# A graph network on one core: relational convolutions over (edge tile, block of 128 destinations) pairs, with edge weights found inside the first one

## The reference, cut to what matters

```python
N, E, D, R, L = 6250, 100000, 128, 8, 3          # dst is sorted; src and etype are random
def rgcn_conv(x, src, dst, etype, bases, comp, root, bias):
    weight = einsum('rb,bio->rio', comp, bases)
    h = einsum('ni,rio->nro', x, weight)
    msg = h[src, etype]                           # one row of 128 for each edge
    cnt = segment_sum(ones(E), dst * R + etype, N * R)
    norm = 1.0 / maximum(cnt[dst * R + etype], 1.0)
    return segment_sum(msg * norm[:, None], dst, N) + x @ root + bias
for l in range(L):                                # batch norm and relu between layers
    ...
x = layernorm(x + rgcn)
h = x @ W_in + b_in                               # 64 wide
for _ in range(3):                                # three hops, rows = src, columns = dst
    cur = segment_sum(cur[dst] * edge_weight[:, None], src, N)
x = layernorm(x + (sum of h and the hops) / 4 @ W_out + b_out)
```

## Time and profile before

| | us |
|---|---|
| median of 3 runs (lowest, highest) | 8620.33 (8615.66, 8631.71) |
| the profiled execution | 8602.98 |
| its span, first to last instruction | 8601.2 |
| POOL busy in it | 5966.9 |
| PE busy in it | 6088.5 |
| DVE busy in it | 5032.0 |

### The profile page before, as it was taken

The page is one execution under the profiler, slowest core; times in us unless marked ns, Lnnn a source line. Parts: engine busy times, 40 slices in busy tenths (PEclk is TensorE's granted clock), DMA queues, the critical chain, the costliest instruction groups (busy, mean ns, idle before and its releaser), DMA issues.

```text
span 8601.2 us, 79809 instructions
## 1 busy us (share of the span) xinstructions
PE 6088.5 (71%) x14111; PEld 2066.8 (24%) x14112; DVE 5032.0 (59%) x12874; ACT 793.9 (9%) x2392; POOL 5966.9 (69%) x5856
## 2 busy tenths in 40 slices
PE   7755047777778788777877867777677777677776
PEld 3233012222222222222222221111111111111111
DVE  8977036666646666636666665555555554555556
ACT  5822000000010000020000010000000000000000
POOL 3877776667777667776667647777677777677774
PEclk9955568888888888888888878889889888898998
DMA  5100011111241111241111211111211111211112
GB/s 192 25 4 1 1 26 46 47 46 46 51 130 46 47 46 46 43 141 46 47 46 47 46 32 24 23 23 23 29 23 24 24 23 23 36 23 23 23 24 30
DMA packets 239252, 354.33 MB, mean 41 GB/s; under 512 B 129737, under 2 KB 139802, under 8 KB 238414
## 3 DMA queue, kind: packets, MB, share of 16 engines
q0 software_dynamic: 180352, 239.74, 13.8%
q1 hardware_dynamic: 58396, 109.81, 3.8%
q10 hardware_dynamic: 130, 0.80, 0.0%
HBM read 258.83 MB, written 100.66 MB: 42 GB/s over the span
## 4 chain that ended last, share of the span: by engine, by line
PE 45%; issue 19%; POOL 18%; DVE 8%; another core or an unknown queue 7%; DMA 2%; DVEq 1%; POOLq 0%; ACT 0%; SPq 0%
PE psum L771 43%; POOL placed_src L454 11%; POOL msg L471 7%; DVE sel L1075 2%; DVE agg L1091 2%; DMA msg<-hop_table,stage_idx 2%; PE psum L755 1%; DVEq L1086 1%; DVE bufD L1081 0%; POOL stage_addr L449 0%; DVE bufE L931 0%; DVE node_stats L1152 0%; DVE bufD L1082 0%; DVE cur L1168 0%
## 5 line engine op out<-in xcount | busy, mean ns | idle before, releaser
L771 PE MATMUL psum<-sel,msg 128*128 128x512 f32 (+1 forms) x9672 | 5148.1, 669 | 2117.8 <-issue 1095.7
L1091 DVE TENSOR_TENSOR agg<-agg,psum 128x512 f32 (+1 forms) x2418 | 1642.1, 679 | 3306.5 <-PE psum L771 1607.5
L471 POOL DMA_INDIRECT msg<-hop_table,stage_idx x2418 | 2486.5, 1028 | 1094.6 <-issue 631.5
L471 POOL DMA_INDIRECT msg<-msg_table,stage_idx x2418 | 2414.2, 998 | 1050.3 <-issue 628.1
L771 PEld LDWEIGHTS psum<-sel,msg 128*128 128x128 f32 (+1 forms) x9672 | 1554.0, 177 | 4882.8 <-issue 3752.6
L1075 DVE TENSOR_SCALAR sel<-iota,slots,norm 128x512 f32<-128x512 f32 x2418 | 1304.1, 564 | 12.5 <-ACT agg L576 12.5
L454 POOL DMA_INDIRECT placed_src<-stage_pay,stage_addr x800 | 1022.0, 1278 | 304.9 <-issue 216.2
L1075 DVE TENSOR_SCALAR sel<-iota,slots 128x512 f32<-128x512 f32 x2418 | 1096.5, 492 | 0.1
L505 ACT CAST stage_idx<-slots 128x4 int32<-128x4 f32 x1212 | 232.9, 194 | 6979.9 <-DMA msg<-msg_table,stage_idx 3526.3
L755 PEld LDWEIGHTS psum<-bufD 125*49 125x49 f16 x918 | 95.5, 104 | 842.8 <-issue 683.0
L1122 DVE SCALAR_TENSOR_TENSOR cur<-iota,bufE,psum 128x128 f32<-128x128 f32 x808 | 234.6, 345 | 88.4 <-PE psum L703 56.9
(11 more groups left out here) (176 smaller groups left out, 1613.0 us busy)
## 6 DMA issues: line engine op xcount, KB each, us to landing
msg_table<-sel SPq DMA_DIRECT2D x147, 512.0 KB
msg<-msg_table,stage_idx POOLq DMA_INDIRECT x2418
msg<-hop_table,stage_idx POOLq DMA_INDIRECT x2418
placed_src<-stage_pay,stage_addr POOLq DMA_INDIRECT x800
placed_dst<-edge_rows SPq DMA_DIRECT2D x13, 781.2 KB
hop_table<-sel SPq DMA_DIRECT2D x21, 224.0 KB, 2.8
bufE<-inv_sqrt SPq DMA_DIRECT2D x2, 1568.0 KB, 10.1
out<-cur SPq DMA_DIRECT2D x12, 256.0 KB
```

Source lines behind the costliest of these rows:

```text
L471: g.indirect_dma_start(out=msg[:, b, 0:width], out_offset=None, in_=table, in_offset=bass.IndirectOffsetOnAxis(ap=stage_idx[:, b:b + 1], a ...
L771: t.matmul(psum[0:width, b // 2 % PB, :], msg[:, b, 0:width], sel[:, b % SB, :], start=b % 2 == 0, stop=b % 2 == 1).then_inc(summed, 1)
L1091: v.tensor_tensor(at, at, psum[0:width, q % PB, :], ALU.add).then_inc(added, 1)
```

## The change

The relational convolutions go over visits. The sorted edges stay packed: `NET` = 782 tiles of 128. A visit is a pair of an edge tile and a block of 128 destinations that the tile reaches; a tile that spans a block's end is visited twice, and there are `NV` = 830 visits for any input. `plan_visits` finds each visit's tile and block on DVE and PE; POOL gathers the visits' tiles from `edge_rows` with 7 indirect DMAs. The selection is 128 by 128 (`visit_sel`, 16 buffers), the product 128 columns, four visits to a PSUM bank; each visit is added to `agg` by itself, at a column unpacked from `visit_pack`. The 13 copies by SP are gone, and so is the separate stage of edge weights: in the first convolution DVE makes one-hot rows of the type alone (24 columns), and one instruction (L1182) writes the weighted selection and `norm` together. POOL takes the gather's indices straight from `visit_src`. `CUTS` is now (6, 34, 42, 50): 6 turns, the 7 tile gathers, 28 turns, then 8 and 8 between layers. The histogram of destinations takes 49 steps of DVE in place of 13. The degree steps go with every third visit.

```diff
-CUTS = (38, 44, NSI)
+NET = -(-E // 128)
+NV = NET + NBLK - 1
+MV = 16
+SV = 16
+MAIN = (0, 1, 6)
+CUTS = (6, 34, 42, NSI)
@@ SP
-                for j in range(NB):
-                    sp.dma_start(placed["dst"][bass.ds(to, E), :]...).then_inc(moved, 16)
-                    sp.wait_ge(moved, 16 * (j + 1))
@@ POOL
+            def visit(k):
+                if k == 0:
+                    pool.wait_ge(visits_ready, 1)
+                for v in range(NV):
+                    n = visits(k, v)
+                    if n >= MV:
+                        pool.wait_ge(visit_summed, n - MV + 1)
+                    g.indirect_dma_start(out=msg[:, n % MV, :], out_offset=None, in_=msg_table,
+                                         in_offset=bass.IndirectOffsetOnAxis(ap=visit_src[:, v:v + 1], axis=0)).then_inc(visit_in[n % MV], 16)
...
+            pool.wait_ge(visits_planned, 1)
+            for j in range(VB):
+                g.indirect_dma_start(out=runs[:, j, :, :]..., in_=edge_rows.rearrange("(t e) w -> t (e w)", e=128), ...)
+            place("src", CUTS[0], CUTS[1])
@@ PE
+                for c in range(NQ):
+                    if k == 0:
+                        if c + 2 < NQ:
+                            turn_types(c + 2)
+                        if c + 1 < NQ:
+                            spread_weights(c + 1)
+                    sums(c)
@@ DVE
-            for j in range(NB):
+            for j in range(NBLK):
                 link(v.tensor_scalar(in_bucket, bucket_f, float(j), 0.0, ALU.is_equal, ALU.add, accum_out=hist[:, j:j + 1]))
...
+                def select(c):
+                    if k == 0:
+                        dve.wait_ge(weight_rows, c + 1)
+                    for j, at in enumerate(chunk_of(c)):
+                        if n >= SV:
+                            dve.wait_ge(visit_summed, n - SV + 1)
+                        if k == 0:
+                            v.scalar_tensor_tensor(out=to, in0=iota[:, 0:128], scalar=low, in1=psum[:, 2 + c % 2, j * 128:(j + 1) * 128],
+                                                   op0=ALU.is_equal, op1=ALU.mult, accum_out=norm[:, at:at + 1]).then_inc(visit_ready, 1)
+                        else:
+                            v.tensor_scalar(to, iota[:, 0:128], low, norm[:, at:at + 1], ALU.is_equal, ALU.mult).then_inc(visit_ready, 1)
...
+                def add(c):
+                    columns = block_columns(dve, c)
+                    dve.wait_ge(visit_summed, visits(k, chunk_of(c)[-1]) + 1)
+                    for j, at in enumerate(chunk_of(c)):
+                        if n:
+                            dve.wait_ge(visit_added, n)
+                        to = agg_and[:, bass.ds(columns[j], 128)]
+                        v.tensor_tensor(to, to, psum[:, bank_of(k, c), j * 128:(j + 1) * 128], ALU.add).then_inc(visit_added, 1)
...
-            edge_weights()
```

572 lines of the change are left out of this document (307 added, 265 removed).

## The result

| | kernel before | changed kernel |
|---|---|---|
| median of its runs | 8626.0 us (4 runs) | 8752.7 us (4 runs, 8748.7 to 8763.9) |
| ratio, 95% interval | | 1.0150 (1.0132 to 1.0167) |
| the profiled execution's span | 8601.2 us | 8747.0 us |

The change makes the kernel slower by 1.5%. The prediction was 8465 us, faster, with a range from 8310 to 8730 us: wrong in sign, and the measured time lies outside the range.

What follows compares the result with a forecast made beforehand. POOL was taken as one unbroken chain from 118 us to the third layer's end. Its terms, -103 + 10 - 10 + 102 - 22 - 65 - 67 = -155 us, gave 8448 us profiled, 8465 us as median; range 8310 to 8730 us.

Steps and rivals of the forecast that it cites:

- Placing before the first convolution: Before the first convolution: 64 fewer POOL scatters at 1.60 us each, -103 us.
- disturbance: Before the first convolution: POOL's scatters no longer slowed during the edge-weight stage, -10 us; in each convolution 15 us remain.
- The stage of edge weights is worth nothing: Before the first convolution: removing its 428 us gains nothing by itself, since POOL's scatters run on until 1171 us.
- Boundaries: Between layers: 32 more scatters each time at 1.60 us, hidden by nothing, 51 us twice, +102 us.
- The convolutions: Three layers: 830 gathers at 1.25 us plus disturbance and smaller waits, giving -22, -65 and -67 us.
- DVE's time a visit: In the convolutions: about 1.0 us, with 0.25 for the selection; 1.15 to 1.25 us in the first.
- Layer 1's extra: First convolution: POOL waits 80 us for buffers, against 35 us in layers 2 and 3.
- Tail: Hops, layer norms and the end: unchanged, 0 us.
- the pace belongs to the gather: Rival, convolutions: a gather takes 1.433 us whatever its followers do; +34, +36, +34 us, 8723 us; chance 0.14.
- The chain of additions: Rival, convolutions: DVE's small additions at L1204 become the bound; +90, +92, +90 us, 8891 us; chance 0.12.
- The waits vanish: Rival, convolutions: PE and DVE never hold POOL; -102, -100, -102 us, 8315 us; chance 0.22.
- signs of being wrong: Layers 2 and 3: idle beyond issue gaps 100 us or more; layer/830 at 1.39 us or more; POOL waiting for the table.

Runs made afterwards that it cites:

- e10: Changed kernel with 32 message buffers, 32 selection buffers and seven PSUM banks in layers 2 and 3: 8826.3 us, ratio 1.0156 to the kernel before.
- e2: Changed kernel with each chunk's four additions at fixed places behind one wait, no packed columns or register steps on DVE: 8772.1 us, ratio 1.0109.
- e3: Changed kernel with one 512-column addition a chunk, no packed columns or register steps on DVE: 8754.8 us, ratio 1.0095.
- e4: Changed kernel with one more product of zeros per visit on PE in layers 2 and 3: 8823.3 us, ratio 1.0171.
- e1: Changed kernel without the visits' selections, products and additions in layers 2 and 3: 8688.1 us, ratio 1.0018; those layers 1135.7 and 1135.0 us.
- e5: e1 with each gather of layers 2 and 3 fetching 64 rows instead of 128: 8692.8 us, long gathers again 1.400 us apart.
- e6: Kernel before without selections, products and additions in layers 2 and 3: 8599.1 us, ratio 0.9884; those layers 1107.8 and 1105.1 us.
- e8: e1 with SP to issue an 8 KB transfer for every gather in layers 2 and 3: 9181.4 us.
- e16: Changed kernel unchanged, run again on the fifth chip: 8002.5 us, ratio 1.0087 to the kernel before at 7932 us.
- e17: Kernel before unchanged, on the sixth chip: 7915.6 us, convolutions of 1011.5, 1014.5 and 1010.8 us.
- e18: e1 repeated on the sixth chip: all three layers at 1.248 to 1.249 us a gather.
- e11: Changed kernel; layer 1 without types and edge weights, layer 2 with products only, layer 3 without additions: 1202.2, 1178.7 and 1182.6 us.
- e12: Changed kernel with POOL also writing one column of zeros behind every gather in layers 2 and 3: 8793.9 us.

## Why the prediction was wrong

By its own steps:

- **Placing before the first convolution, -103, and disturbance, -10: right.** 608 scatters took 1053.4 us, 96 and 448 took 186.3 and 759.6: -107.5 us. The seven tile gathers kept POOL busy for 1.90 us each, and took 15.1 us with their gaps against the 10 forecast. The first gather began at 1082.5 us, forecast 1068.
- **The stage of edge weights is worth nothing: right.** Its 428 us went, and the start moved by what the scatters did.
- **Boundaries, +102: right,** 102.7, and 207 us from last to first gather where 208 stood.
- **The convolutions, -22, -65, -67: wrong,** +69, +35, +35. The step that failed is "Against today's 1155 that leaves 117 us for disturbance and waits; a layer gains only as far as these shrink", with what follows: the waits were sized at 80, 35 and 35 us because PE and DVE get less to do and 16 buffers cover a stall of 7 us. The waits came out at 188, 150 and 152 us; disturbance, put at 15 us a layer, at 2 us or less. Their place was right, POOL does wait for PE and PE for DVE. Their cause was not. On the first chip DVE's instructions are held up in stretches (407 us of idle time with nothing to wait for in one layer, last section; 344 us in e10, on the fourth), and that does not shrink with the work: fewer or cheaper additions (e2, e3), a higher clock (e4) and more room (e10) left a layer at 1183 us or more. Nor would a perfect follower have helped: with none at all POOL itself is held to 1.400 us a gather (e1, e5, e6, e8). On two other chips the same kernels run at 1.25 us with no wait (e16, e17, e18). So less work for PE and DVE, by 40% and 29% of their busy time, bought almost nothing, and the 24 further visits cost their full pace: 24 x 1.43 = 34 us a layer, which is what layers 2 and 3 show.
- **DVE's time a visit:** the selection of 128 columns was put at 0.25 us and took 0.36. It decided nothing, since on the fifth chip DVE keeps up.
- **Layer 1's extra, forecast as 45 us more waits than in the others: right in kind.** It is 36 us longer than layer 2, and e11 takes 35 us of it away with the types and weights.
- **Tail, 0:** -6.8 us.

Without the limit the change would still lose. From e17 to e16 (two chips, both without it) the start gives -86.7 us, the convolutions +25.0, +24.9 and +28.3, the boundaries +103.1 and the tail -5.4, together +89.2 us. 24 gathers more at 1.249 are 30 us, and 3 to 6 us come back by gathers of 0.944 to 0.948 us instead of 0.951. So of the 146 us on the first chip, some 89 are work that the change adds to POOL's chain, and the other 57 go with that chip's limit. On the fifth chip the changed kernel is slower by 0.9% (e16), on the first by 1.5%.

Of the rivals, **the pace belongs to the gather** had the numbers for layers 2 and 3 (+36 and +34), and half of the mechanism. The pace does stay when the followers are cut, but at 1.400 us and not 1.433; with followers POOL waits for PE, as the first account said; and on two chips the pace is 1.25 us. That 1.433 fits so well is in part luck. Its 8723 us came out 43 us short in the profiled execution: 35 us by layer 1, 14 by the start, less 7 at the tail. I gave it 0.14, because "PE psum L771" stood in the row of POOL's waits, 82 us of it. The fact in its favour was in the same argument: a hop with 80 us less of PE's work took the same time, and I had read it as "PE is not simply the bound" and stopped there. **The chain of additions** fell with e2 and e3: L1204 takes 0.287 us and 0.57 from start to start, near the forecast of 0.3 and 0.5. The rule of the Trainium skill, "VectorE: DVE Perf Modes", section "The TRN2 errata — SBUF-src ops pay a fixed extra latency per instruction", gives 0.29 us, and the trace agrees with 0.287. Removing the chain gains 0.4 to 0.6%. **The waits vanish** is what the last two chips show of the mechanism, and even there the changed kernel is slower, since the kernel before gains more by it.

Two of the signs of being wrong that the prediction named came true: a layer's length divided by 830 was to be 1.39 us or more and is 1.431, and the idle time beyond the issue gaps was to be 100 us or more in layers 2 and 3 and is 150. The third did not; POOL never waited for the table.

## What to carry to other kernels

When different amounts of follow-up work give the same stage time, suspect something that they share: here it was neither PE's nor DVE's work. Before a gain is booked for taking work from an engine that another one waits for, look at why it is late. An engine that is late because it is busy gains by less work; one that stands still with nothing to wait for may not. How long data lies ready before it is used says who is behind (14 us here, 0.47 us on another chip). Run the bound engine's own stream with the followers cut, and long enough: in e1 the first 186 gathers looked free. And run the kernel before on more than one chip before a figure of a single trace becomes a rule. A change that only makes idle engines idler must be charged, at the measured pace, for every instruction that it adds to the engine in front: here 72 gathers and 7 tile gathers.

## What was not expected of the hardware

The kernel before took 8626 us on the first chip and 7932 us on the fifth, and the difference is in how the instructions flow, not in the work. In layer 2 of the changed kernel, first chip, some 450 of DVE's 3240 recorded sequencer steps took over 0.5 us, more than 410 of them 0.65 to 0.72, in stretches of some 4 to 13 us; on the fifth chip (e16) there is none. (The kernel before has none either, on the first chip or the sixth.) DVE's timeline shows the holes that they leave:

```profile
2699.01 0.60 DVE L1185 TENSOR_SCALAR sel<-iota,agg_and 128x128 f32<-128x128 f32 x2
2704.91 0.29 DVE L1204 TENSOR_TENSOR agg_and<-agg_and,psum 128x128 f32 x1 [5.29 <-issue]
2707.74 0.29 DVE L1204 TENSOR_TENSOR agg_and<-agg_and,psum 128x128 f32 x1 [2.55 <-issue]
```

One sequencer step of that kernel over all its 624 times, min/median/max ns, on the first chip and then on the fifth (e16):

```profile
L338 DVEq FUSED_REGOPS  x624: 4/190/1205, 480.9 to 5110.3; - x156
```

```profile
L338 DVEq FUSED_REGOPS  x624: 190/190/190, 478.9 to 4617.1; - x156
```

So three engines show the same figure: DVE's held steps take 0.65 to 0.72 us, SP's waiting instruction in e8 took 0.70, and SP's instructions and POOL's gathers in e1 and e8 come 1.400 us apart, twice 0.70. That one cause stands behind all three is likely by this and not shown.

What the limit is stays open. It is not in rows or bytes (e5), not in POOL's own time (e12), not in the transfers, which land 2.2 to 2.3 us after their start on every chip, and not in POOL alone, since SP and DVE are held too. It sets in when POOL is 25 to 28 us ahead of it, as if something filled up (e1, e5, e8).

One more difference between the chips goes with it. Each gather raises its semaphore 16 times. In e18, on the sixth chip, the trace holds a record of each of the 16; in the long gathers of e1 it holds 2 of the 16. The changed kernel's whole trace has 94937 such records of transfers on the fifth chip and 30380 on the first, for the same transfers. All traces of the first four chips are short of them, and none of the last two is. So where time is lost, records are lost too, and a rival account is that the recording of the profile itself holds the engines on those chips. The Trainium skill, "NOTIFIC — the notification-queue block", section "7.1 Overflow: three behaviours, one of which stalls the engine", says that the block which writes the engines' event records holds its producers back when its own pipeline is full, rather than lose a record inside it; the held engines would fit that, and the missing records would have to be lost elsewhere. Its section "10. Constraints, capacities, measured rates" says that a record costs the engine no cycles, at the rates that were tried. No run here decides: every execution timed here was a traced one, as its granted clock shows. If the recording is the cause, some 57 of the 146 us and the gap of 8% between the chips would not exist in an execution without it, and the change would still lose by what the fifth and sixth chip show.
